# Counts of the last three edge groups made beside the dense products instead of in the build stage, with 21 instead of 23 additions per mixing tile

## What is computed

```python
h = relu(layernorm(x))
W = zeros(1024, 1024).at[src, dst].add(edge_weight)   # edges with src or dst of 1024 and more fall away
x = x + h @ W.T + bias
h = relu(layernorm(x))
# two layers: nb(h)[d] = mean of h[src] over the edges with dst == d
h1 = relu(h @ W_self0 + nb(h) @ W_neigh0 + b0)
x = x + h1 @ W_self1 + nb(h1) @ W_neigh1 + b1
```

## Time and profile before

| what | value |
|---|---|
| median of 3 runs | 827.85 us (827.69 to 829.63) |
| the profiled execution, its own time | 828.25 us |
| its span in the trace | 826.5 us |
| PE busy | 793.4 us, 96% of the span |
| DVE, ACT, POOL busy | 480.2, 371.0, 387.8 us |
| mean granted PE clock | 0.991 of full speed |

### The profile page before, as it was taken

The page is one execution under the profiler, slowest core; times in us unless marked ns, Lnnn a source line. Parts: engine busy times, 40 slices in busy tenths (PEclk is TensorE's granted clock), DMA queues, the critical chain, the costliest instruction groups (busy, mean ns, idle before and its releaser), DMA issues.

```text
span 826.5 us, 13468 instructions
## 1 busy us (share of the span) xinstructions
PE 793.4 (96%) x4612; PEld 642.9 (78%) x4613; DVE 480.2 (58%) x800; ACT 371.0 (45%) x483; POOL 387.8 (47%) x558
## 2 busy tenths in 40 slices
PE   3999999999969999999999999999999999999998
PEld 2666787888848887888887878888877888878786
DVE  7999678777522687866623353232556757336443
ACT  6755643433234232232327886543222323256653
POOL 3000055556745678856762220114878676724311
PEclk9999999999979999999999999999999999999999
DMA  3122356765466673566965653555853669758654
GB/s 108 43 69 81 98 169 201 234 213 182 151 204 209 225 233 116 173 201 209 329 231 169 193 191 102 179 167 175 276 171 115 198 212 326 253 186 276 208 171 137
DMA packets 84566, 152.61 MB, mean 185 GB/s; under 512 B 11125, under 2 KB 22508, under 8 KB 84496
## 3 DMA queue, kind: packets, MB, share of 16 engines
q1 hardware_dynamic: 62794, 103.72, 39.7%
q10 hardware_dynamic: 20182, 43.07, 14.9%
q0 software_dynamic: 1520, 4.92, 1.5%
HBM read 104.41 MB, written 47.27 MB: 184 GB/s over the span
## 4 chain that ended last, share of the span: by engine, by line
PE 61%; POOL 13%; issue 8%; DMA 7%; DVE 5%; ACT 3%; POOLq 2%; SPq 1%; ACTq 0%; DVEq 0%
PE bank L1341 33%; PE bank L1369 19%; POOL AT L813 8%; DMA stage<-hT_scratch 3%; PE bank L1177 3%; PE bank L1188 3%; DMA az<-asum_scratch 2%; POOL T L866 2%; POOL T L868 2%; POOL S L833 1%; PE bank L1172 1%; ACT split L1036 1%; DVE L L1553 1%; POOLq L813 1%; PE bank L1385 1%
## 5 line engine op out<-in xcount | busy, mean ns | idle before, releaser
L1341 PE MATMUL bank<-slot,split 128*128 128x512 f32 x1680 | 388.8, 393 | 9.7 <-issue 7.9
L1341 PEld LDWEIGHTS bank<-slot,split 128*128 128x128 f32 x1680 | 315.7, 189 | 77.4 <-issue 11.5
L813 POOL TENSOR_TENSOR AT<-AT,az 128x50 int32 (+3 forms) x288 | 89.4, 310 | 142.7 <-DMA az<-asum_scratch 99.2
L851 POOL TENSOR_TENSOR split<-stage,split 128x512 fp32r<-128x512 f32 x50 | 64.5, 1291 | 138.4 <-ACT split L1036 138.4
L1659 DVE TENSOR_TENSOR slot<-T,slot 128x512 fp32r<-128x512 f32 x64 | 71.8, 1122 | 89.6 <-ACT slot L1027 85.1
L1068 ACT CAST Ax<-AT 128x1280 fp32r<-128x1280 uint16 x40 | 106.3, 2659 | 32.3 <-PE bank L1369 21.6
L1276 PE MATMUL bank<-slot,split_m 128*128 128x512 f32 x320 | 91.3, 396 | 0.0
L1027 ACT CAST slot<-T 128x512 fp32r<-128x512 f32 x64 | 39.8, 622 | 107.4 <-POOL T L868 80.6
L1659 DVE TENSOR_TENSOR slot<-wst,slot 128x512 fp32r<-128x512 f32 x48 | 47.1, 1007 | 57.2 <-ACT slot L1027 57.1
L1369 PE MATMUL bank<-slot,Ax 128*128 128x512 f32 x320 | 77.2, 394 | 0.5 <-ACT Ax L1068 0.4
L1770 DVE SCALAR_TENSOR_TENSOR cst<-bank,dinv,stage 128x512 f32<-128x512 f32 x40 | 30.1, 751 | 73.9 <-PE bank L1369 73.4
(11 more groups left out here) (176 smaller groups left out, 1028.1 us busy)
## 6 DMA issues: line engine op xcount, KB each, us to landing
stage<-hT_scratch SPq DMA_DIRECT2D x90, 256.0 KB, 3.7
wst<-in_L_gnn_W_neigh SPq DMA_DIRECT2D x56, 256.0 KB, 4.1
wst<-in_L_gnn_W_self SPq DMA_DIRECT2D x56, 256.0 KB, 3.1
x1b_scratch<-x ACTq DMA_DIRECT2D x10, 512.0 KB, 5.4
hT_scratch<-hTs ACTq DMA_DIRECT2D x10, 512.0 KB, 3.0
stage<-prod0s_scratch SPq DMA_DIRECT2D x20, 256.0 KB, 2.9
hT_scratch<-h1s ACTq DMA_DIRECT2D x20, 256.0 KB, 2.8
stage<-prod1s_scratch SPq DMA_DIRECT2D x20, 256.0 KB, 2.8
```

What stands on the lines that cost most here:

```text
L813: pool.tensor_tensor(a, a, az32[:, n % NZ, pairs * pos:pairs * (pos + 1)], ALU.add) \
L851: pool.tensor_tensor(split[:, v % 2, 1, :], source(v), split[:, v % 2, 0, :].bitcast(F32), ALU.subtract).then_inc(s_olo, 1)
L1341: last = pe.matmul(dense_bank(v, which)[:, :], split[:, v % 2, a, NT * k:NT * (k + 1)], slot[t % 2][:, b, HF * (HK * which + k):HF * (HK * ...
```

## The change

The counts of groups 37 to 39 (LATE = 37, LG = 3) are no longer made in the build loop. Their one-hot tiles `R_late` and `L_late` are made by DVE in iterations 1 to 3 of the dense stage (`late_rows`), PE multiplies them behind products 2, 3 and 4 (`late_sums`, 8 matmuls each, with no weights), ACT copies the sums from PSUM banks 6 and 7 straight into `az` as two units of four windows each (`late_sums_out`), and POOL adds eight windows in each of iterations 3, 4 and 5. These units no longer go through DRAM. The weights of these groups are left to the loop for further ranges: for a late group that has a destination under 1024, `general` widens the range so that the loop takes all its windows; for this data it adds nothing. Mixing tiles get 21 additions each, 14 follow in iterations 0 to 2 (4, 5, 5), and the degrees begin one iteration later. The total stays 288 additions, and the units that go through DRAM fall from 45 to 40.

```diff
-SLOT_PAD = 112
 TIERS = sorted(set(WDS))[1:]
-STARTS = [(j, c) for j in range(NG) for c in range(0, GC, SHARED[j])]
+LATE = 37
+LG = NG - LATE
+EARLY_STARTS = [(j, c) for j in range(LATE) for c in range(0, GC, SHARED[j])]
+STARTS = EARLY_STARTS + [(j, c) for j in range(LATE, NG) for c in range(GC)]
...
-OFFW, BASEW, START, COLS = 0, 8, 12, 20
+OFFW, BASEW, COLS = 0, 8, 12
...
-BASES = {0: range(4, 8), 8: range(8, 16), 15: range(16, 32), 31: range(32, 40)}
+BASES = {0: range(4, 8), 8: range(8, 16), 15: range(16, 32), 31: range(32, LATE)}
...
-SETS = [(0, 8), (8, 11), (11, 13), (13, 15), (15, 17)] + [(j, j + 1) for j in range(17, NG)]
+SETS = [(0, 8), (8, 11), (11, 13), (13, 15), (15, 17)] + [(j, j + 1) for j in range(17, LATE)]
...
-MIX_ADDS = 23
-FIRST_DEG = 6
+MIX_ADDS = 21
+LATE_AT = 2
+FIRST_DEG = 7
...
+UNITS += [[(j, c) for c in range(b, b + GC // 2)] for j in range(LATE, NG) for b in (0, GC // 2)]
...
-FIRST_ADD += [IN_MIXING + (NWIN - IN_MIXING) * v // PAIRS for v in range(PAIRS + 1)]
+FIRST_ADD += [IN_MIXING + (len(EARLY_STARTS) - IN_MIXING) * v // (LATE_AT + 1) for v in range(LATE_AT + 2)]
+FIRST_ADD += [len(EARLY_STARTS) + GC * u for u in range(1, LG + 1)]
...
+        late = ExitStack()
+        sb("beside_late", [P, 15488], F32, late)
+        R_late = sb("R_late", [EP, GC, P], BF16, late)
+        L_late = sb("L_late", [EP, GC, KA], BF16, late)
+        late.close()
...
+            sp.wait_ge(s_start, 1)
+            sp.dma_start(tab[:, :, :], tab_s[:, :]).then_inc(s_tabs, 16)
...
-                    if pos == 0:
+                    if pos == 0 and n < NS_A:
                         pool.wait_ge(s_az[n % NZ], used(n, NZ))
+                    elif pos == 0:
+                        pool.wait_ge(s_late, n - NS_A + 1)
...
+            act.copy(slo2_late[:, :, :, :], twice(slo[:, LATE:NG, :], LG)).then_inc(s_slate, 1)
...
+            def late_sums_out(u):
+                for n in (NS_A + 2 * u, NS_A + 2 * u + 1):
+                    act.wait_ge(s_at, windows_to(n - NZ + 1))
+                    act.wait_ge(s_plate, u + 1)
+                    act.copy(az[:, n % NZ, 0:unit_cols(n)], late_bank(n)[:, 0:unit_cols(n)]).then_inc(s_late, 1)
...
+                    if 0 <= v - LATE_AT < LG:
+                        late_sums_out(v - LATE_AT)
...
+                    pe.matmul(general_sums(), ones[:, 0:EP], general_d[:, :], start=True, stop=True)
...
+            def late_sums(u):
+                pe.wait_ge(s_hlate, u + 1)
+                if u == 0:
+                    pe.wait_ge(s_ht, TN)
+                else:
+                    pe.wait_ge(s_late, 2 * u)
+                for n in (NS_A + 2 * u, NS_A + 2 * u + 1):
+                    for c in range(GC // 2):
+                        chunk = GC // 2 * (n - NS_A - 2 * u) + c
+                        last = pe.matmul(late_bank(n)[:, KA * c:KA * (c + 1)], R_late[:, chunk, :], L_late[:, chunk, :],
+                                         start=True, stop=True)
+                last.then_inc(s_plate, 1)
             def degrees(k):
                 if k == 0:
-                    pe.wait_ge(s_ht, TN)
+                    pe.wait_ge(s_late, 2 * LG)
...
+                if 0 <= v - LATE_AT < LG:
+                    late_sums(v - LATE_AT)
...
-            dve.wait_ge(s_alone, 2 + len(SHARES) + len(TIERS))
-            dve.tensor_scalar(tab_g[:, START:START + GC], first[:, :], narrow[:, 0:1], None, ALU.subtract) \
-                .then_inc(s_tab, 1)
...
+            def late_with_weights():
+                link(dve.tensor_scalar(general[:, :], base_w[:, :], float(F), float(WD * TN), ALU.is_lt, ALU.mult))
+                return tick(dve.tensor_scalar(general_d[:, :], ident[0:NG, LATE:NG], general[:, 0:1], None, ALU.mult))
...
+            def span_of_groups(marked):
+                highest = tick(dve.tensor_reduce(high[:, :], dst_g[:, :, :], AX_X, ALU.max))
+                dve.wait_ge(s_dve, marked)
+                dve.wait_ge(s_alone, 2 + len(SHARES) + len(TIERS))
+                link(dve.tensor_reduce(general[:, :], general_d[:, :], AX_X, ALU.add))
+                narrowed = tick(dve.scalar_tensor_tensor(out=narrow[:, :], in0=general[:, :], scalar=1.0 / TN,
+                                                         in1=narrow[:, :], op0=ALU.mult, op1=ALU.add))
+                dve.wait_ge(s_dve, highest)
+                spread_done = tick(dve.tensor_tensor(spread[:, :], high[:, :], first[:, :], ALU.subtract))
+                dve.wait_ge(s_dve, narrowed)
+                dve.tensor_scalar(tab_s[:, :], first[:, :], narrow[:, 0:1], None, ALU.subtract).then_inc(s_start, 1)
+                dve.wait_ge(s_dve, spread_done)
...
+                dve.tensor_copy(tier_of[:, LATE:NG], general_sums())
+                dve.tensor_tensor(key2_late[:, :, :, :], twice(key[:, LATE:NG, :], LG),
+                                  general_sums().unsqueeze(2).unsqueeze(3).to_broadcast([EP, LG, GC, 2]), ALU.add)
...
+            def late_rows(u):
+                if u == 0:
+                    dve.wait_ge(s_slate, 1)
+                else:
+                    dve.wait_ge(s_plate, u)
+                hot_keys(L_late[:, :, :], key2_late[:, u, :, :], WD)
+                hot_rows(R_late[:, :, :], slo2_late[:, u, :, :]).then_inc(s_hlate, 1)
...
+                if 0 <= v - LATE_AT + 1 < LG:
+                    late_rows(v - LATE_AT + 1)
```

More of the change, by code:

```diff
@@ L169, in build_program @@
         tab_g = sb("tab_g", [NG, COLS], I32, build)
+        tab_s = sb("tab_s", [NG, GC], I32, build)
+        general = sb("general", [NG, 1], F32, build)
+        general_d = sb("general_d", [NG, LG], F32, build)
         tab_ag = sb("tab_ag", [NG, GC], I32, build)
@@ L974, in _ @@
             act.wait_ge(s_tabw, 16)
-            for j in range(NG):
+            for j in range(LATE):
                 for i in range(2):
```

66 lines of the change are left out of this document (38 added, 28 removed).

## The result

| | median, us | lowest to highest | executions |
|---|---|---|---|
| before | 829.54 | 827.69 to 831.39 | 13 |
| changed | 823.16 | 818.41 to 825.97 | 13 |

The ratio is 0.9917, with a 95% interval of 0.9897 to 0.9936. The change makes the kernel faster by 6.4 us, where 12.0 was forecast, and 823.16 lies outside the range of 811.0 to 820.5. The profiled execution is the one of 818.41 us, the fastest of the 13 (span 816.3), so it flatters the change: profile against profile, the difference is 9.84 us.

What follows compares the result with a forecast made beforehand. PE was taken as the bound, busy 793.4 of 826.5 us. Terms -7.2 + 0.7 - 4.7 - 2.8 + 1.2 + 0.8 = -12.0 us gave a forecast of 816.0 us, range 811.0 to 820.5.

Steps and rivals of the forecast that it cites:

- build: Build loop: three groups fewer save 7.2 us of PE time, added small DVE operations cost 0.7; -6.5 us.
- gap: PE's wait before product 0: shrinks from 7.9 to 3.2 us as POOL finishes its additions earlier; -4.7 us.
- clock in the first products: First two products after the gap: granted clock stays up, 10.98 us instead of 13.72; -2.8 us.
- product 7: Dense stage: late copies and additions on ACT and POOL delay this product's operand once; +0.8 us.
- The degrees one iteration later end at iteration 16, before `AT_TOP`; they cost nothing beside the products: Dense stage: moving the degrees one iteration later was claimed to cost 0.
- Afterwards POOL's spare time is small but positive, so the lag isn't repeated: Dense stage after product 7: POOL's lateness was claimed to cost nothing further.
- Rival 3: Iterations 4 to 8: POOL's backlog is larger and block sums come late; 818.2, or 820.5 if passed on; chance 0.1.
- since it was still up 3.2 us into the old one: Gap before product 0: ground for claiming the clock survives a 3.2 us gap, worth -2.8 us.
- rival 2: Before product 0: the gap shrinks too little to keep the clock; 818.8, or 819.8 with more lag; chance 0.17.
- wait behind weight block 7: Mixing: fewer units precede this load in SP's queue, so POOL waits for its next unit until 173.0.
- rival 1: Before product 0: POOL catches up and the gap closes, saving 3.2 us more; 812.8; chance 0.2.
- the 1.8 us by that rule: Dense stage: with additions at 0.49 us from GpSimd and VectorE contention, product 7 is late by 1.8 instead of 0.8.

Runs made afterwards that it cites:

- e14: The changed kernel again with nothing altered, one profiled execution: 821.35 us.
- e1: The changed kernel again with nothing altered: median 822.29 us, ratio 0.9920; its profiled execution took 824.10 us.
- e4: The changed kernel with the late groups one iteration earlier (products 1, 2 and 3): 820.12 us, ratio 0.9908.
- e5: The changed kernel with all work on the late groups left out, so its output differs from the reference's: 818.83 us, ratio 0.9872.
- e7: The changed kernel with PE taking each degree sum one product later: 822.33 us, ratio 0.9917.
- e8: The changed kernel with 20 additions per mixing tile and PE's degrees one product later: 822.00 us, ratio 0.9901.
- e6: The changed kernel with 20 additions per mixing tile instead of 21: 819.73 us, ratio 0.9882.
- e12: The changed kernel with 24 unused transposes of the identity on PE ahead of product 0: 822.68 us, ratio 0.9920.
- e9: The changed kernel with 25 additions in each of the first five mixing tiles and 17 in each of the last five: 818.26 us, ratio 0.9872.
- e10: The changed kernel with the 25 and 17 split of additions and the late groups one iteration earlier: 815.73 us, ratio 0.9835.
- e3: The changed kernel with operands 0 and 1 loaded and their remainders made ahead of most last-tile additions: 818.35 us, ratio 0.9870.
- e13: The changed kernel again with nothing altered, one profiled execution: 821.56 us.
- e15: The kernel of e12 again, one profiled execution: 824.53 us.
- e11: The kernel before with its additions split 27 and 19 instead of 23 in each mixing tile: 827.23 us, ratio 0.9977.
- e16: The kernel of e12 again, another profiled execution: 821.57 us.

## Why the prediction was wrong

The direction was right, and so was the mechanism of the build, of the gap and of product 7. One cost was missing, the clock was taken as safer than it is, and so the size was wrong. The terms by three profiles of the changed kernel, each against the profile before (from the rows of PE's timeline and the table above, rounded):

| term | forecast | 818.41 us | e14, 821.35 us | e1, 824.10 us |
|---|---|---|---|---|
| build | -6.5 | -7.1 | -6.9 | -6.5 |
| gap | -4.7 | -5.1 | -4.5 | -3.1 |
| clock in the first products | -2.8 | -2.6 | -1.0 | -0.9 |
| three late batches | +1.2 | +1.3 | +1.3 | +1.3 |
| product 7 | +0.8 | +0.7 | +0.7 | +0.7 |
| degrees and what stands with them | 0 | +3.4 | +2.4 | +3.2 |
| behind product 10 | 0 | -0.8 | +0.8 | +0.9 |
| span, in all | -12.0 | -10.2 | -7.2 | -4.5 |

The medians differ by 6.4 us. The first profile came nearer to the forecast by luck: it kept the clock, and is 0.8 us shorter behind product 10, where the change explains nothing and the two others are longer.

**The step that failed** is "The degrees one iteration later end at iteration 16, before `AT_TOP`; they cost nothing beside the products", and with it "Afterwards POOL's spare time is small but positive, so the lag isn't repeated". They cost 3.4 us in the first profile, 3.2 in e1 and 2.4 in e14 (from product 7 at 268.13 to product 10 at 287.75, less the 17.23 us of before). The prediction looked at where the degrees end, not at who feeds them where they begin. The additions that made product 7 late by 0.7 also held back `T`, so ACT's rounding, so DVE, behind whose work the degree sums stand in just these iterations. Nor was the lag gone in the iterations after: DVE's third block came 8.5 us behind the start of product 7 (274.23 and 265.69), where before it was 5.9 (284.43 and 278.49), so it was still 2.6 us late. Rival 3 had half of it: it names ACT, "which waits for them ahead of rounding", and prices 818.2 to 820.5, but stops at ACT. e4 and e5 show the cause (take the additions out of iteration 5, or leave them out, and the waits go). Both also move or remove ACT's copies and the late matmuls, but by the changed kernel's trace ACT had nothing to do for 5.51 us before POOL's sums came, so it is POOL that was late. e7 and e8 show that the place of the degrees is worth about 1 us of it at most: in e7 the waits move from `degs` to `split` and `cst`.

**The clock** is the second. The step "since it was still up 3.2 us into the old one" reads one execution as a bound. It stayed up behind 2.82, 2.38 (e6) and 2.70 us (e8), and fell behind 2.69 (e4), 2.70 (e7), 3.02 (e5), 3.39, 3.76 and 4.78. That term was worth -2.6 at best and -0.9 to -1.2 in three profiles of four, so rival 2, at 0.17, should have been the forecast's own case. By e12 its share is still the smaller one.

Two sums of the prediction are off by 0.1 to 0.2 us and change nothing. Seven small operations at 0.19 us less one of 0.22 are 1.1 us, not 1.2. And the 2.8 us of the clock compare 13.72 with 10.98; a row of the same 48 matmuls at full clock is 11.13, which gives 2.6.

**What was right.** The gap: the forecast put the weight load at 169.7, the next unit's arrival at 173.0, the operand load at 217.4, POOL's remainder at 224.0 and product 0 at 225.5. SP's queue in the changed kernel has

```profile
169.12 0.33 SPq L652 DMA_DIRECT2D wst<-in_L_gnn_W_self  x1
169.55 47.18 SPq L718 DMA_DIRECT2D az<-asum_scratch  x21
216.82 0.86 SPq L670 DMA_DIRECT2D stage<-hT_scratch  x2
```

and POOL

```profile
172.90 5.62 POOL L842 TENSOR_TENSOR AT<-AT,az 128x40 int32 x14 [0.85 <-DMA az<-asum_scratch]
...
222.94 2.50 POOL L880 TENSOR_TENSOR split<-stage,split 128x512 fp32r<-128x512 f32 x2
```

So the wait behind weight block 7, which the prediction held against rival 1, is there, at 172.90. e9 and e10 show the way out that rival 1 wanted: with more additions early, POOL begins on the operands at 221.52 and 220.93, before mixing ends. The size of the gap still differs between executions by 2 us. In e1 POOL's remainder comes at 225.65, 2.7 us after that of the first profile; POOL took up the first unit behind the weight load at 174.28, not 172.90 (1.4 us), and most of what is left arises here, where the same row of the first profile has 0.92 us of idle time:

```profile
215.60 5.64 POOL L842 TENSOR_TENSOR AT<-AT,az 128x50 int32 x16 [2.42 <-issue]
```

The additions themselves are not slower (POOL is busy with them for 75.9 us between 100 and 224 in the one, 76.6 in the other). What makes "issue" longer in one execution than in another, POOL's register loads or something else, no run separates.

**The additions' price.** In iteration 3 eight of them took 4.29 / 8 = 0.54 us each, with DVE busy for 2.57 of the 4.29 us; in iterations 4 and 5 they took 2.82 / 8 = 0.35. The Trainium skill (GPSIMD Engine Reference, Specifications) has GpSimd contend with VectorE instructions of two SBUF inputs. The trace agrees in iteration 3, where DVE ran `TENSOR_TENSOR` instructions on `wst` and `slot` and on `iota` and the late keys. In iteration 5, the one that decides, DVE was idle because it waited for POOL's own chain, so the lower price held and the 1.8 us by that rule did not come.

## What to carry to other kernels

When work is put into the slack of one chain, follow every engine's queue behind it until it is empty again. The operand path had room for the additions, but the same additions delayed the block sums, and the longest waits were those of a small instruction four steps further that nobody counts as part of that path; one iteration earlier the same work cost 2.1 us instead of 3.5 to 4.3. And where an engine is late at a boundary, try the order of its work before its amount: 25 and 17 additions instead of 21 and 21 brought a gap of 2.8 to 4.8 us to 0 and 0.6, where 20 and 20 left 2.4 us.

## What the runs showed that I had not expected

- The granted clock fell after waits as short as 1.84 us (e3) and stayed up after one of 2.82 us. It also fell in the build in some executions, around 44 to 48 us in e5, e9, e13 and e15 (0.72 over the window of e13 above), and at 33 to 36 us in e1, e8, e11 and e16 (0.50 to 0.53). In e13 mixing ended 1.3 us later for it than in e14, and 1.6 later than in the first profile, though PE had no longer wait than 1.27 us just before, the same as in the first profile, which kept the clock.
- Executions of the changed kernel differ by up to 7.6 us, 0.9% (818.41 to 825.97). Those of the kernel before kept within 3.7 us beside them (827.69 to 831.39), but spread over 6.8 us in 17 executions on another chip (826.23 to 833.02), so the spread is not the change's alone. The first profile happened to be the fastest of 13. A comparison of two single profiles would have said 9.84 us, and hidden that the clock falls more often than not (in three profiles of four). The version e10, whose gap is 0.57 us and which doesn't wait for the operand of product 7, keeps within 2.9 us, in 5 executions only.
